# Two-layer graph network on 100,000 nodes: edge work of layer 1 packed into the loop's first half, sums over gathered h rows moved into its second half, last phase without gathers, relu written in PSUM

## The reference

```
def sage(x, W_l, b, W_r):            # edges (src, dst), sorted by dst
    agg  = segment_sum(x[src], dst)  # 100000 nodes, 25000 edges, 256 features
    mean = agg / max(degree, 1)
    return mean @ W_l + b + x @ W_r
h1  = relu(sage(x,  W1_l, b1, W1_r))
h2  = relu(sage(h1, W2_l, b2, W2_r))
out = layernorm(x + h2 @ W3 + b3)    # over the 256 features
```

## Time and profile before

| | |
|---|---|
| median of three runs | 2995.66 us |
| profiled execution, span from first to last instruction | 2989.1 us |
| time around the span | 6.6 us against the median of the runs |
| busy: PE, DVE, ACT, POOL | 96%, 82%, 67%, 72% of the span |
| mean granted TensorE clock | 0.992 of full speed |

### The profile page before, as it was taken

How to read it: one execution, slowest core, us unless ns; L and a number is a source line. 1 busy time by engine, 2 the same in 40 slices (tenths; PEclk the granted TensorE clock), 3 DMA queues, 4 the chain that set the end, 5 groups by cost and what they waited for, 6 DMA issues and landing times. The chain is left out here.

```text
span 2989.1 us, 55620 instructions
## 1 busy us (share of the span) xinstructions
PE 2869.4 (96%) x18457; PEld 2581.4 (86%) x18457; DVE 2445.0 (82%) x4001; ACT 1997.4 (67%) x2992; POOL 2151.1 (72%) x1732
## 2 busy tenths in 40 slices
PE   5999999999999999999999999999999989999996
PEld 4888989898888889898988888898989879888885
DVE  5787887879787878878787878788787879899896
ACT  3676766767676767667676767676676746555554
POOL 5777777777776767667777767677777747777776
PEclk9999999999999999999999999999999999999998
DMA  4444444444444445444444444444444366666663
GB/s 131 151 152 145 162 150 149 154 142 161 152 155 148 153 143 165 149 148 154 143 159 154 155 147 153 145 164 149 148 154 145 130 205 232 235 223 226 238 221 141
DMA packets 253121, 488.25 MB, mean 163 GB/s; under 512 B 37615, under 2 KB 165206, under 8 KB 253090
## 3 DMA queue, kind: packets, MB, share of 16 engines
q1 hardware_dynamic: 202498, 387.58, 38.6%
q0 software_dynamic: 50176, 99.91, 10.3%
q10 hardware_dynamic: 416, 0.40, 0.0%
HBM read 284.67 MB, written 206.22 MB: 164 GB/s over the span
## 5 line engine op out<-in xcount | busy, mean ns | idle before, releaser
L487 ACT ACTIVATE h_full<-pair,bias 128x512 f32<-128x512 f32 x784 | 531.6, 685 | 681.2 <-PE pair L861 666.4
L649 DVE TENSOR_TENSOR h_lo<-h_full,h_hi 128x1024 fp32r<-128x1024 f32 x392 | 651.7, 1663 | 188.3 <-ACT h_hi L489 188.2
L391 POOL TENSOR_TENSOR xb<-xn,b_row 128x1024 f32<-128x1024 f32 x196 | 471.5, 2405 | 297.7 <-DVE y L671 295.9
L345 POOL DMA_INDIRECT xe<-in_x_dram,e_stage x392 | 500.9, 1278 | 176.9 <-issue 97.7
L872 PE MATMUL pair<-w_hi,h_hi 128*128 128x256 f32 x1960 | 565.4, 288 | 26.6 <-DVE h_lo L649 24.5
L872 PE MATMUL pair<-w_lo,h_hi 128*128 128x256 f32 x1960 | 555.3, 283 | 0.0
L872 PE MATMUL pair<-w_hi,h_lo 128*128 128x256 f32 x1960 | 555.2, 283 | 0.0
L489 ACT CAST h_hi<-h_full 128x1024 fp32r<-128x1024 f32 x392 | 412.0, 1051 | 12.5
L872 PEld LDWEIGHTS pair<-w_hi,h_hi 128*128 128x128 f32 x1960 | 375.6, 192 | 51.7 <-DVE h_lo L649 47.7
L500 ACT ACTIVATE o<-y,nb,rs 128x256 f32<-128x256 f32 x784 | 407.2, 592 | 5.6 <-DVE nb L702 5.3
L861 PE MATMUL pair<-xt_hi,w_hi 128*128 128x512 f32 x980 | 401.6, 410 | 7.9 <-DVE xt_lo L645 4.3
(11 more groups left out here) (124 smaller groups left out, 6439.6 us busy)
## 6 DMA issues: line engine op xcount, KB each, us to landing
xn<-in_x_dram SPq DMA_DIRECT2D x196, 512.0 KB, 4.0
out_dram<-o SPq DMA_DIRECT2D x196, 512.0 KB, 2.6
seg<-seg_tab SPq DMA_DIRECT2D x74, 512.0 KB, 5.1
xdb_tab<-xdb SPq DMA_DIRECT2D x49, 512.0 KB, 4.8
h_tab<-src_h SPq DMA_DIRECT2D x49, 512.0 KB
h_tab<-dst_h SPq DMA_DIRECT2D x49, 512.0 KB, 6.3
xn<-h_tab SPq DMA_DIRECT2D x49, 512.0 KB, 5.1
xb<-xdb_tab SPq DMA_DIRECT2D x49, 512.0 KB, 4.1
```

The lines of the kernel that those rows point to most:

```text
L345: nc.gpsimd.indirect_dma_start(out=xe[:, kind, s], out_offset=None, in_=x, in_offset=bass.IndirectOffsetOnAxis(ap=e_stage[:, kind, s:s + 1 ...
L391: nc.gpsimd.tensor_tensor(xb[:, b], xn[:, u], b3_row[:, :].unsqueeze(1).to_broadcast([P, S, D]), ALU.add).then_inc(xb_ok, 1)
L487: nc.scalar.activation(h_full[:, n, k], ps[:, k], ACT.Relu, bias=bias[:, n, k:k + 1]).then_inc(hf_ok[n], 1)
L649: nc.vector.tensor_tensor(h_lo[:, h], h_full[:, n], h_hi[:, h].bitcast(f32), ALU.subtract).then_inc(hlo_ok[n], 1)
```

## The change

- The edge groups of layer 1 run two to an iteration, from group 2 to the middle of the loop (`stage`, `LAG`, `HB`). The 48 matmuls of the destinations move to the even group after.
- In the second half of the loop the sources' h1 rows are gathered from `h_tab` into `xe`, PE turns them (`turn_sums`, 4 transposes to a group of rows), DVE scans them (`sum_up_again`, one scan to a group), and SP stores the sums to a new DRAM table `run_tab`. The last two edge groups of this are done in steps 0 and 1 of the last phase (`LEFT` = 2).
- The last phase loads those sums (`load_run`) instead of gathering rows, so PE makes 8 transposes a step instead of 16, DVE no scans, POOL only scatters. The loads of the first two steps and the first means move into the loop's last iteration.
- ACT writes bias and relu back into PSUM; `h_full` is gone, and high and low part of h are read from PSUM.
- The orders of all queues are rewritten, in the last phase as below. The indices of indirect transfers are read in place, without the copies to `e_stage` and `t_stage`. The start is reordered: W1_r comes first and is split alone, the first two groups of rows begin before the edge indices are made, and those are loaded by six transfers on SP instead of nine on ACT.

```
+        def stage(i, u, part):
+            h = i * 2 + u // 2
+            layer1 = part == "layer1" or (part == "first" and u >= 2)
+            finish = u % 2 == 0 and (part == "layer1" or (part == "turn" and u == 0))
+            sums = part in ("sums", "last") or (part == "turn" and u >= 2)
+            return h - LAG, h - HB, layer1, finish, sums
...
+            def load_hd(j, b):
+                if early(j, 2):
+                    sp.wait_ge(xt_ps, (NG - 1 + j) * K)
+                    sp.wait_ge(xb_ok, NG - 1 + j)
+                after(sp, c_hd_ps, (j - 1) * K)
+                sp.dma_start(xn[:, 2 + b], slots_of(h_tab, j)).then_inc(c_hd_in[b], 16)
...
+            def load_run(j, b):
+                if early(j, 2):
+                    sp.wait_ge(xb_ok, NG - 3 + j)
+                sp.wait_ge(run_out[b], slot_use(j, b))
+                after(sp, c_mean_ok, j - 1)
+                sp.dma_start(xn[:, b].rearrange(flat), runs_of(j)).then_inc(c_run_in[b], 16)
+                sp.dma_start(deg_of[:, b * G:(b + 1) * G], seg_row(j, 1)).then_inc(c_deg_in[b], 16)
...
+            def load_xb(j, b):
+                if early(j, 2):
+                    sp.wait_ge(y_ok, NG - 1 + j)
+                after(sp, c_y_ok, j - 1)
+                sp.dma_start(xb[:, b], slots_of(xdb_tab, j)).then_inc(c_xb_in[b], 16)
...
             def step(j, b, left):
+                if left:
+                    load_xb(j + 1, 1 - b)
+                if early(j, LEFT):
+                    store_run(NE - LEFT + j, (NE - LEFT + j) % 2)
+                if early(j - 1, 2) and j >= 1:
+                    store(NG - 3 + j, (NG - 3 + j) % 2)
                 if left > 1:
-                    load(j + 2, b)
-                if left:
-                    load_x(j + 1, 1 - b)
+                    load_hd(j + 2, b)
+                    load_run(j + 2, b)
...
             def high_h(g, n, h, ps):
                 for k in range(K):
                     act.wait_ge(l_ps[n], g * K + k + 1)
-                    after(act, hlo_ok[n], g)
-                    nc.scalar.activation(h_full[:, n, k], ps[:, k], ACT.Relu, bias=bias[:, n, k:k + 1]).then_inc(hf_ok[n], 1)
+                    nc.scalar.activation(ps[:, k], ps[:, k], ACT.Relu, bias=bias[:, n, k:k + 1]).then_inc(hf_ok[n], 1)
                 act.wait_ge(hf_ok[n], (g + 1) * K)
-                nc.scalar.copy(h_hi[:, h], h_full[:, n]).then_inc(hhi_ok[n], 1)
...
             def step(j, b, left):
                 if left:
                     dst_high(j + 1, 1 - b)
-                if isinstance(j, int) and j == 0:
-                    for n in range(2):
-                        act.wait_ge(y_out[n], 16 * (NG // 2))
-                if not (isinstance(j, int) and j < 3):
+                    mean_high(j + 1, 1 - b)
+                if early(j, 3):
+                    if j:
+                        normalise(NG - 3 + j, (NG - 3 + j) % 2)
+                else:
                     finish_edges(j - 3, 1 - b)
-                second(j, 0)
-                if left:
-                    mean_high(j + 1, 1 - b)
-                second(j, 1)
+                second(j, b, 0)
+                second(j, b, 1)
                 second_high(j, b)
-                if not (isinstance(j, int) and j < 2):
+                if early(j, 2):
+                    deviation(NG - 2 + j, (NG - 2 + j) % 2)
+                else:
                     deviation_edges(j - 2, b)
                 if not left:
...
             def step(j, b, left):
-                early = isinstance(j, int) and j < 2
-                if not early:
+                g = NG - 2 + j if early(j, 2) else None
+                if g is None:
                     residual_edges(j - 2, b)
-                if not (isinstance(j, int) and j < 3):
-                    factors_edges(j - 3, 1 - b)
+                else:
+                    residual_rows(g, g % 2, pair[1] if j == 0 else pair[3])
+                if early(j, 1):
+                    low_h(NG - 1, 1, 2, pair[3])
+                else:
+                    low_second(j - 1, 1 - b)
                 if left:
-                    scan(j + 1, 1 - b)
-                    low_dst(j + 1, 1 - b)
                     means(j + 1, 1 - b)
-                if not early:
-                    sums(j - 2, b, c_y_ok, c_stats_ok)
+                    low_hd(j + 1, 1 - b)
+                if g is None:
+                    sums_edges(j - 2, b)
+                else:
+                    sums_of(g, g % 2, y_ok, stats_ok)
                 if left:
                     mean_low(j + 1, 1 - b)
-                if not early:
+                if g is None:
                     averages_edges(j - 2, b)
-                low_second(j, b)
+                else:
+                    averages(g, g % 2, stats_ok, mv_ok)
+                if early(j, LEFT):
+                    n = NE - LEFT + j
+                    for k in range(K):
+                        sum_up_again(n, n % 2, k, pair[0])
+                if early(j, 3):
+                    if j:
+                        factors_rows(NG - 3 + j, (NG - 3 + j) % 2)
+                else:
+                    factors_edges(j - 3, 1 - b)
                 if not left:
+                    low_second(j, b)
                     factors_edges(j - 2, b)
                     for n, c in ((j - 1, 1 - b), (j, b)):
...
+            def sum_up_again(j, b, k, ps):
+                dve.wait_ge(mask_in[b], slot_use(j, b))
+                dve.wait_ge(hs_ps, j * K + k + 1)
+                if not early(j, 1):
+                    dve.wait_ge(hs_ok, j * K + k - 1)
+                if early(j, 1):
+                    dve.wait_ge(mean_ok, NE)
+                elif not early(j, 2):
+                    dve.wait_ge(run_out[b], slot_use(j - 2, b))
+                nc.vector.tensor_tensor_scan(run[:, b, k], seg[:, b], ps[:, k], run[:, 1 - b, k, G - 1:G], ALU.mult, ALU.add)\
+                    .then_inc(hs_ok, 1)
...
+            def turn_sums(j, b, k, ps):
+                pe.wait_ge(hs_in[b], slot_use(j, b, 16 * S))
+                turn(ps, xe[:, b], k).then_inc(hs_ps, 1)
...
+            def turn_hd(j, b):
+                pe.wait_ge(c_hd_in[b], slot_use(j, b))
+                if early(j, 1):
+                    pe.wait_ge(y_ok, NG - 2)
+                after(pe, c_hdlo_ok, j)
+                for k in range(K):
+                    turn(pair[0], xn[:, 2 + b], k).then_inc(c_hd_ps, 1)
...
             def step(j, b, left):
                 if left:
-                    turn_edges(j + 1, 1 - b)
-                if isinstance(j, int) and j == 0:
-                    pe.wait_ge(y_ok, NG)
+                    if early(j, LEFT + 1) and j:
+                        pe.wait_ge(hs_ok, (NE - LEFT + j) * K)
+                    turn_hd(j + 1, 1 - b)
                 pe.wait_ge(c_mlo_ok, j + 1)
                 pe.wait_ge(c_hdlo_ok, j + 1)
-                after(pe, c_hf_ok, j * K)
+                if early(j, 1):
+                    pe.wait_ge(y_ok, NG - 1)
+                after(pe, c_hlo_ok, j - 1)
                 for m in range(K):
-                    columns([(X2R, xe_hi[:, b], xe_lo[:, b]), (X2L, xt_hi[:, b], xt_lo[:, b])], pair[2], m).then_inc(c_l2_ps, 1)
-                if not (isinstance(j, int) and j == 0):
-                    last_layer(j - 1, 1 - b, c_hlo_ok, c_y_ok, c_l3_ps)
+                    columns([(X2R, xe_hi[:, b], xe_lo[:, b]), (X2L, xt_hi[:, b], xt_lo[:, b])], pair[1 + b], m).then_inc(c_l2_ps, 1)
+                if early(j, LEFT):
+                    n = NE - LEFT + j
+                    pe.wait_ge(c_hdlo_ok, j + 2)
+                    for k in range(K):
+                        turn_sums(n, n % 2, k, pair[0])
+                if early(j, 1):
+                    third_layer(NG - 1, pair[3])
+                else:
+                    last_layer(j - 1, 1 - b)
                 if not left:
-                    last_layer(j, b, c_hlo_ok, c_y_ok, c_l3_ps)
+                    last_layer(j, b)
             edge_passes(pe, step)
...
```

More of the change, by code:

```diff
@@ L114, in build @@
[L114 to L120, removed]
@@ L258, in body @@
-                    if u == 0 and not first:
-                        edge_store(i - 1, 3)
-                    if not (first and u < 2):
-                        store(g - 2, u % 2)
[L262 to L268, removed]
-            sp.wait_ge(dst_out, 16 * NE)
-            sp.wait_ge(src_out, 16 * NE)
@@ L286, in load_x @@
-            def load_x(j, b):
-                after(sp, c_y_ok, j - 1)
-                sp.dma_start(xb[:, b], slots_of(xdb_tab, j)).then_inc(c_xb_in[b], 16)
-            load(0, 0)
-            sp.wait_ge(c_hs_in[0], 16 * S)
-            load(1, 1)
-            sp.wait_ge(y_ok, NG)
-            load_x(0, 0)
-            sp.wait_ge(y_out[0], 16 * (NG // 2))
-            store(NG - 1, 1)
-            def step(j, b, left):
+                    if part == "first" and u == 1:
+                        sp.wait_ge(prep, PREP_RDEG)
```

(32 more changed lines are left out.)

971 lines of the change are left out of this document (505 added, 466 removed).

## The result

The changed kernel takes 3358.85 us (median of 4 runs, 3356.79 to 3360.31) against 2996.18 for the kernel before (4 runs, 2994.37 to 2997.53): a ratio of 1.121, 95% interval 1.120 to 1.123. Forecast were 3332 us, a ratio of 1.112, with 3205 to 3400 as the range. The time is 27 us, 0.8%, above the point.

The account below looks back on a forecast made before the run. PE was taken to bound the loop, and a ring through SP, DMA and PE the last phase: 2413 + 12 + 870 + 10.5 + 19.5 = 3325 us of span, with 6.6 added 3332; range 3205 to 3400.

Parts of the forecast that it names:

- The ring: Last phase: residual, SP's issues of xb and hd, hd's landing, PE's work to the next residual; 18.5 us, 47 times, 870.
- the last term: In the ring: PE's transposes, layer 2 and layer 3 up to the next residual, 9.47 us plus 1.8 for the clock.
- That nothing else lengthens the ring: Last phase: means, high and low parts and ACT's normalising fill the ring's 16.7 us without lengthening it.
- rival 3: Last phase: the clock stays high, 16.7 us a step, 3247 us in all; chance inside the main case's 0.82.
- The loop: PE's work sets it: 57.7 us an iteration in the first half, 38.7 in the second; 2359 plus 20 of stalls.
- The start: Before the loop's full pace: PE loses 27 us instead of 40, bounds 15 and 40.
- the turn between the halves: Middle of the loop: fetch of h rows waits for the last look-up and store of dst_h; 7 us exposed.
- The turnover: From the loop's end to the residual of the last group in step 0: 12 us, the former 20 gone.
- The end: Last ring's residual to that of group 48, 10.5 us, then 19.5 us behind it.
- Rivals 1 and 2: Last phase: 1, a DVE and ACT ring, 11.1 us a step, chance 0.07; 2, PE's work alone, 9.25, chance 0.03.
- rival 4: Last phase: the clock stays low through the step, 26 us a step, 3684 us; chance 0.05, including a clock between.
- rival 5: Loop: DVE or POOL bounds one half, 1 us more a group, up to 150 us on top; chance 0.03.

Follow-up runs that it names:

- the pair of kernels: Changed kernel with DVE's factors moved to just behind the residual, without and with 48 needless matmuls in PE's pause: 3338.23 and 3262.05 us.
- the kernel with the pause filled: Changed kernel with 48 needless matmuls in PE's pause before each wait for hd, DVE's factors not moved: 3325.55 us, ratio 1.107.

## Why the prediction was right, step by step

**The ring** was right in its place, its members and its size: 886.6 us for 47 rings against 870. Its terms add up to 18.46, rounded to 18.5, and measure 18.86: of the 0.40 between, 0.30 is in the last term (11.57 - 9.47 = 2.1 instead of 1.8), 0.14 in the landing, and SP's issues give 0.04 back. The last term alternates: the way from transposes to residual takes some 12.1 and 11.0 us in turn, the half level lasting 5.3 us behind PE's resumption in the step shown and 2.7 in the one before it. Half of that time is the loss, 2.7 and 1.4, on average the 2.0 that the pair of kernels shows in the same term. So the 2.1 is the clock, but for 0.1. In the working of the clock the 3.44 us of 16 transposes is a duration and the 1.67 beside it is from start to start; the like of 3.44 is 1.91. The 1.8 doesn't rest on it but on the 3.7 us of half level.

**That nothing else lengthens the ring** came true, but by a narrow margin. Means, factors and normalising were said to fill the ring of 16.7 without lengthening it; in fact they close a ring of their own, of 17.5 by the kernel with the pause filled, one microsecond behind the one that bound. In the changed kernel it stayed hidden: 46 of the 47 rings ended with the residual waiting for PE, only the first with a wait for ACT (2.20 us). Had the clock stayed high (rival 3), it would have bound: the kernel with the pause filled took 3325.55 us, not that rival's 3247. The part of the prediction that gave it room was right only because the clock fell.

**The loop** came out as added up: two groups of the first half take 28.9 us (57.8 an iteration, 57.7 predicted), one of the second half 9.71 (38.8 against 38.7), and PE is busy without a gap in both windows above. The 20 us of stalls allowed for were not there; the loop's last matmul ended at 2398, 15 us before the 2413 forecast. The start lost about 30 us instead of 27, the turn between the halves 8 to 9 instead of 7. Relu in PSUM was rightly taken as free for ACT (664 ns a relu against 685), but its gain was the surprise: the earlier trace rows gave a loss of 1.0 us an iteration, and all of it went.

**The turnover** was the undersized term outside the ring: from the end of the loop to the residual of the last group it took 33 us (2398 to 2431.26) instead of 12. That the residual was only 6.3 us behind the 2425 forecast is luck: the 15 us that the loop had in hand covered most of the 21 missing here. PE stood still for 9.6 us before hd of group 0:

```profile
2395.01 1.23 DVE L625 TENSOR_TENSOR y<-pair,xb 128x1024 f32<-128x1024 f32 x1 [0.18 <-PE pair L921]
...
2397.40 0.95 POOL L414 DMA_INDIRECT xe<-h_tab,h_row  x1 [0.30 <-issue]
2398.37 4.64 POOL L373 TENSOR_TENSOR xb<-xn,b_row 128x1024 f32<-128x1024 f32 x2
2400.80 0.38 SPq L274 DMA_DIRECT2D xn<-h_tab  x1
...
2407.61 1.97 PE L901 MATMUL pair<-ident,xn 128*128 128x128 f32 x8 [9.56 <-DMA xn<-h_tab]
```

load_hd(0) reuses a tile that POOL still has to read for group 194; POOL's read waits for the residual of 193 and stands 2.1 us behind four issues of fetch; the load then lands 6.8 us behind its issue. I had counted the work of the turnover, not the chain that its first load hangs on. That moving the fetch would help was not tried.

**The end**: from the last ring's residual to that of group 48 it took 3334.18 - 3317.86 = 16.3 us instead of 10.5. That way goes over DVE's and ACT's queues, which had no slack left: PE waited 3.4 us for the residual of group 47, and the last residual 2.22 for ACT. Behind it came 20.7 us (19.5 predicted). The four misses, 6.3 (loop and turnover, net) + 16.6 + 5.8 + 1.2, are the 30 us between the spans 3325 and 3354.9.

**The rivals.** Rivals 1 and 2 are real mechanisms of this kernel, and each became the bound as soon as what lay above it was taken away: 10.83 a step (11.1 forecast) and 9.21 (9.25). Rival 3 is refuted by the granted clock of 0.77 in the last phase, rival 4 by the windows above, where it is back at 1.00 within the step, rival 5 by PE's full windows in the loop.

## What to carry to other kernels

Read the order of an in-order DMA queue as part of the dependence graph: a load behind one that waits for the end of the step starts at the end of the step, whatever it needs itself. Sum the ring from each gated issue back to its own gate, and every other ring through that issue, before counting the work that was saved; work counts only once no ring is longer. When a change that must save work comes out slower, swap the issues first.

## What the runs showed of the hardware

- Adding work made a kernel faster: 48 needless matmuls in each pause of PE took 76 us off (3338.23 to 3262.05); the granted clock stayed at 1.00 instead of 0.78. With PE waiting some 7 us a step the clock fell to its half level about 2.2 us into the pause shown, and the eight transposes behind it took 1.96 us instead of 1.04.
- DVE's subtraction of two SBUF tiles took 2.66 us at 1203.17 in the kernel before, while POOL ran an addition from 1202.35 on, and the next such subtraction 1.23 at 1207.18, when POOL had no addition running; with one input in PSUM it took at most 1.23 in 392 cases, and the kernel 39 us less (2992.06 to 2952.82). The Trainium skill (SBUF — State Buffer, section "Who interferes with whom") states that a DVE instruction with two SBUF inputs contends with a GpSimd instruction that reads SBUF, and one with a single SBUF input doesn't; the trace agrees.
- The same load woke PE 4.8 to 6.9 us behind its issue within one kernel, 6.1 to 6.9 in the first three rings, mostly 4.8 to 5.6 in the others.
